# Attention scores from split operands: three one-pass products, with the keys split a batch ahead on ScalarE and GpSimd

## What is computed

```python
x = x + jnp.tanh(g_xattn[0]) * _L0_xattn_ref(_layernorm(x, axis=-1), ctx_1024, ...)
x = x + jnp.tanh(g_ffn[0]) * _L0_ffn_ref(_layernorm(x, axis=-1), ...)
x = x + jnp.tanh(g_xattn[1]) * _L1_xattn_ref(_layernorm(x, axis=-1), ctx_1024, mask_BxS2_bf1, ...)
x = x + jnp.tanh(g_ffn[1]) * _L1_ffn_ref(_layernorm(x, axis=-1), ...)
```

```python
sim = jnp.einsum('bhid,bhjd->bhij', q, k) * scale
attn = jax.nn.softmax(sim, axis=-1)
out = jnp.einsum('bhij,bhjd->bhid', attn, v)
...
return out @ Wo + bo
```

## Time and profile before

| | |
|---|---|
| median of three runs | 1489.21 us |
| span of the profiled execution, first to last instruction | 1487.2 us |
| the profiled execution's own time beyond its span | not listed; median less span is 2.0 us |
| PE busy | 1444.1 us, 97% of the span |
| DVE, ACT, POOL busy | 72%, 62%, 43% |
| granted TensorE clock, mean | 0.999 of full speed |
| first attention, feed-forward, second attention, spiking block | about 15 to 614, to 738, 749 to 1349, to 1487 us |

### The profile page before, as it was taken

How to read it: one execution, slowest core, us unless ns; L and a number is a source line. 1 busy time by engine, 2 the same in 40 slices (tenths; PEclk the granted TensorE clock), 3 DMA queues, 4 the chain that set the end, 5 groups by cost and what they waited for, 6 DMA issues and landing times. The chain is left out here.

```text
span 1487.2 us, 27490 instructions
## 1 busy us (share of the span) xinstructions
PE 1444.1 (97%) x9366; PEld 1209.9 (81%) x9384; DVE 1064.9 (72%) x2311; ACT 923.1 (62%) x1924; POOL 640.4 (43%) x755
## 2 busy tenths in 40 slices
PE   9999999999999999879999999999999999999997
PEld 8888888888888887639978888888888888778886
DVE  5677877666767678798566666666767676776887
ACT  4666666666666665496456666666666666556663
POOL 1333344343433334556023434343333333455885
PEclk9999999999999999999999999999999999999999
DMA  7655544444444442300055444444444444320011
GB/s 226 192 178 161 165 132 153 137 145 144 140 146 138 153 130 85 91 1 1 12 183 165 135 157 133 157 129 161 134 159 132 154 129 151 109 79 8 29 35 43
DMA packets 202786, 182.70 MB, mean 123 GB/s; under 512 B 12368, under 2 KB 201808, under 8 KB 202640
## 3 DMA queue, kind: packets, MB, share of 16 engines
q1 hardware_dynamic: 202080, 180.91, 38.7%
q10 hardware_dynamic: 576, 0.13, 0.1%
HBM read 95.74 MB, written 85.25 MB: 122 GB/s over the span
## 5 line engine op out<-in xcount | busy, mean ns | idle before, releaser
L1131 POOL TENSOR_TENSOR PN<-E,RC 128x512 f32<-128x512 f32 x378 | 331.2, 904 | 491.9 <-DVE RC L1089 491.9
L1038 DVE TENSOR_REDUCE MX<-pS 128x6 f32<-128x462 f32 (+1 forms) x384 | 222.6, 580 | 265.4 <-PE pS L657 265.4
L772 ACT ACTIVATE G<-pP 128x308 f32<-128x308 f32 (+1 forms) x488 | 208.9, 428 | 226.8 <-PE pP L525 226.5
L695 PE MATMUL pO<-work,PT 128*128 128x128 f32 (+1 forms) x2560 | 328.3, 276 | 4.1 <-ACT PT L856 4.1
L657 PE MATMUL pS<-G,XT 128*128 128x462 f32 (+1 forms) x768 | 321.0, 507 | 0.0
L695 PEld LDWEIGHTS pO<-work,PT 128*128 128x128 f32 (+1 forms) x2560 | 307.7, 192 | 8.4 <-issue 5.8
L847 ACT ACTIVATE E<-E 128x462 f32<-128x462 f32 (+1 forms) x384 | 209.6, 546 | 136.5 <-DVE E L1048 128.2
L523 PE MATMUL pP<-Chi,Ahi 128*128 128x308 f32 x496 | 235.2, 474 | 1.4 <-ACT G L772 1.2
L1048 DVE TENSOR_TENSOR E<-pS,MX 128x462 f32<-128x462 f32 (+1 forms) x384 | 223.6, 582 | 8.9
L856 ACT ACTIVATE PT<-pT 128x512 f32<-128x512 f32 (+1 forms) x384 | 200.2, 522 | 30.2 <-PE pT L680 28.7
L1086 DVE TENSOR_REDUCE SM<-E 128x16 f32<-128x1232 f32 (+1 forms) x144 | 184.8, 1290 | 44.7 <-ACT E L847 43.6
(11 more groups left out here) (241 smaller groups left out, 2032.7 us busy)
## 6 DMA issues: line engine op xcount, KB each, us to landing
values<-ST SPq DMA_DIRECT2D x256, 256.0 KB
work<-values SPq DMA_DIRECT2D x512, 128.0 KB
values<-ST SPq DMA_DIRECT2D x64, 208.0 KB
work<-values SPq DMA_DIRECT2D x128, 104.0 KB
C<-in_ctx SPq DMA_DIRECT2D x32, 154.0 KB
X<-in_x SPq DMA_DIRECT2D x16, 256.0 KB, 5.0
out<-s_O SPq DMA_DIRECT2D x16, 256.0 KB, 2.3
work<-in_L_xattn_Wq SPq DMA_DIRECT2D x2, 512.0 KB, 5.9
```

The lines of the kernel that those rows point to most:

```text
L695: last = nc.tensor.matmul(pO[:, 0:CH], PT[0:rows, c, :], V[(t - 1) % VRING][0:rows, tile, CH * hh:CH * hh + CH], start=c == 0, stop=c == C ...
L772: return nc.scalar.activation(G[0:live, g % 2, :, head, :], bank[0:live, 0:KEYCOLS].rearrange("p (b k) -> p b k", k=KEYS), ACT.Copy)
L1038: nc.vector.tensor_reduce(MX[:, h0:h1], pS[u][:, 0:(h1 - h0) * KEYS].rearrange("p (h k) -> p h k", k=KEYS), X_AXIS, ALU.max).then_inc(max_ ...
L1131: nc.gpsimd.tensor_tensor(out, e, scale, ALU.mult).then_inc(prob_ready, 1)
```

## The change

- **Scores.** Each f32 score matmul becomes three f32r matmuls into the same bank: `XThi` by `Ghi`, `XTlo` by `Ghi`, `XThi` by `Glo`. The first waits for `ghi_out`, the last for `glo_out`.
- **Keys split.** `G` stays f32 and is filled as before. New buffers `Ghi` and `Glo` hold one batch. ACT copies each unit of the next batch into `Ghi` (`keys_hi`), behind the same unit's exponential in slot t; POOL subtracts (`keys_lo`) at the head of its slot, ahead of the probabilities. In the fourth slot of a group the third unit comes after the last key's copy, and after the tiling of the context on POOL.
- **x split.** The copy of the turned x goes to f32r `XThi`, and DVE subtracts `XTlo` once in a group, in its third slot.
- **Contexts.** The ring of raw contexts has two places (`RAW`); contexts 2 and 3 are loaded once 0 and 1 are turned, behind the query and key weights and two loads of x. In the loop the load of a context waits for the turn of the one two before it.
- **Room.** `XTlo` of the first layer lies in the buffer of the spiking weights, and `WT` in that of `WP`. The DMA that places the mask's row in `G` (second layer) waits for `glo_out` in place of `score_ready`.

```diff
 def load_context(sp, c, dram, g):
-    sp.dma_start(c["C"][0:KEYS, g % CTX, :, :], dram[g * GROUP:(g + 1) * GROUP].rearrange("b k d -> k b d")
-                 ).then_inc(c["c_in"][g % CTX], 16)
+    sp.dma_start(c["C"][0:KEYS, g % RAW, :, :], dram[g * GROUP:(g + 1) * GROUP].rearrange("b k d -> k b d")
+                 ).then_inc(c["c_in"][g % RAW], 16)
...
-            for g in range(CTX):
+            for g in range(RAW):
                 sp.wait_ge(sem["padded"], g + 1)
                 load_context(sp, ctx, ctx_dram, g)
...
+            for g in range(RAW, CTX):
+                sp.wait_ge(ctx["ct_turned"], g - RAW + 1)
+                load_context(sp, ctx, ctx_dram, g)
...
                     if u == 0 and b == 0:
                         pe.wait_ge(xt_out, group + 1)
-                        wait(pe, made_out, MADE[t])
+                        pe.wait_ge(xt_low, group + 1)
                     wait(pe, shifted, (t - 1) * 3 + u + 1)
                     h0, h1 = UNITS[u]
                     out = pS[u][:, 0:(h1 - h0) * KEYS]
-                    if layer == 1 and u == 0 and b == 0:
-                        pe.wait_ge(bias_in[half], 16 * (group // 2 + 1))
-                    nc.tensor.matmul(out, XT[:, half, b, :], G[:, half, b, h0:h1, :].rearrange("p h k -> p (h k)"),
-                                     start=True, stop=True).then_inc(score_ready, 1)
+                    hi, lo = (c[:, h0:h1, :].rearrange("p h k -> p (h k)") for c in (Ghi, Glo))
+                    pe.wait_ge(ghi_out, t * 3 + u + 1)
+                    nc.tensor.matmul(out, XThi[:, half, b, :], hi, start=True, stop=False)
+                    nc.tensor.matmul(out, XTlo[:, half, b, :], hi, start=False, stop=False)
+                    pe.wait_ge(glo_out, t * 3 + u + 1)
+                    nc.tensor.matmul(out, XThi[:, half, b, :], lo, start=False, stop=True).then_inc(score_ready, 1)
...
+            def keys_hi(t, u):
+
+                (h0, h1), b, group = UNITS[u], t % GROUP, t // GROUP
...
+                wait(act, score_ready, (t - 1) * 3 + u + 1)
+                nc.scalar.activation(Ghi[:, h0:h1, :], G[:, group % 2, b, h0:h1, :], ACT.Copy).then_inc(ghi_out, 1)
...
+                def next_hi(u):
+                    if t + 1 < BATCH:
+                        keys_hi(t + 1, u)
+
                 produced(0)
                 produced(1)
                 produced(2)
                 exps(0)
+                next_hi(0)
...
                 produced(3)
                 exps(1)
+                next_hi(1)
                 produced(4)
                 probs_out(0)
                 produced(5)
                 exps(2)
+                if b < GROUP - 1:
+                    next_hi(2)
                 probs_out(1)
                 produced(6)
+                if b == GROUP - 1:
+                    next_hi(2)
                 probs_out(2)
...
+            def x_low(g):
+                dve.wait_ge(xt_out, g + 1)
+                nc.vector.tensor_tensor(XTlo[:, g % 2, :, :].rearrange("p b q -> p (b q)"), pO[:, :],
+                                        XThi[:, g % 2, :, :].rearrange("p b q -> p (b q)").bitcast(F32),
+                                        ALU.subtract).then_inc(xt_low, 1)
...
+            def keys_lo(t, u):
+
+                if t < BATCH:
+                    h0, h1 = UNITS[u]
+                    pool.wait_ge(ghi_out, t * 3 + u + 1)
+                    nc.gpsimd.tensor_tensor(Glo[:, h0:h1, :], G[:, (t // GROUP) % 2, t % GROUP, h0:h1, :],
+                                            Ghi[:, h0:h1, :].bitcast(F32), ALU.subtract).then_inc(glo_out, 1)
...
             for t in range(BATCH):
                 b, group = t % GROUP, t // GROUP
                 nxt = group + 1 < GROUPS
+                keys_lo(t + 1, 0)
+                keys_lo(t + 1, 1)
+                if b < GROUP - 1:
+                    keys_lo(t + 1, 2)
```

More of the change, by code:

```diff
@@ L36 @@
 CTX = 4
+RAW = 2
 FC = FF // 128
@@ L98, in context_buffers @@
          "Vlo": s.enter_context(nc.sbuf_tensor(f"Vlo_{layer}", [128, 2, OCTET], F32R))}
-    c["c_in"] = [s.enter_context(nc.semaphore(f"c_in{i}_{layer}")) for i in range(CTX)]
+    c["c_in"] = [s.enter_context(nc.semaphore(f"c_in{i}_{layer}")) for i in range(RAW)]
     for n in ("ct_turned", "chi_out", "clo_out", "tiled"):
@@ L266, in _ @@
         def _(dve):
-            for i in range(CTX):
+            for i in range(RAW):
                 nc.vector.memset(ctx["C"][:, i, :, :], 0.0).then_inc(sem["padded"], 1)
@@ L355, in attention @@
         XN = sb("XN", [128, GROUP, CH])
-        XT = sb("XT", [128, 2, GROUP, QUERIES])
+        XThi = sb("XThi", [128, 2, GROUP, QUERIES], F32R)
+        XTlo = p["F"][:, :, :].rearrange("p i (b q) -> p i b q", q=QUERIES) if layer == 0 else sb(
+            "XTlo", [128, 2, GROUP, QUERIES], F32R)[:, :, :, :]
+        Ghi, Glo = sb("Ghi", [128, HEADS, KEYS], F32R), sb("Glo", [128, HEADS, KEYS], F32R)
         BN = sb("BN", [128, GROUP, 6])
@@ L426, in attention, with key_made @@
             MADE.append(MADE[-1] + len(products(t)))
+        def key_made(first, head):
+            t = first + head // 4
+            return MADE[t] + products(t).index(("key", head)) + 1
         def probabilities(t, n):
@@ L739, in slot @@
                         pe.wait_ge(xt_out, group + 2)
+                        pe.wait_ge(xt_low, group + 2)
                     if b == 3 and cur and group + CTX < GROUPS:
@@ L767, in x_out @@
                 act.wait_ge(xt_turned, g + 1)
-                nc.scalar.activation(XT[:, g % 2, :, :].rearrange("p b q -> p (b q)"), pO[:, :],
+                nc.scalar.activation(XThi[:, g % 2, :, :].rearrange("p b q -> p (b q)"), pO[:, :],
                                      ACT.Copy).then_inc(xt_out, 1)
+            def keys_hi(t, u):
+                (h0, h1), b, group = UNITS[u], t % GROUP, t // GROUP
+                if t == 0:
+                    for i in range(2):
+                        act.wait_ge(first_out[i], (BLOCKS + h1) // 2)
+                elif b == 0:
+                    act.wait_ge(made_out, key_made(t - GROUP, h1 - 1))
+                if layer == 1 and b == 0 and u == 0:
+                    act.wait_ge(bias_in[group % 2], 16 * (group // 2 + 1))
+                wait(act, score_ready, (t - 1) * 3 + u + 1)
+                nc.scalar.activation(Ghi[:, h0:h1, :], G[:, group % 2, b, h0:h1, :], ACT.Copy).then_inc(ghi_out, 1)
             def keys_out(bank, g, head):
@@ L834, in produced @@
                         if b == 0 and j == 0:
-                            wait(act, score_ready, t * 3)
+                            wait(act, glo_out, t * 3)
                         act.wait_ge(made, m + 1)
@@ L1068, in slot @@
                     context_lo(nc, ctx, pO, group + CTX)
+                if b == 2 and nxt:
+                    x_low(group + 1)
                 row_max(2)
@@ L1159, in _ @@
                 tile_context(nc, pool, ctx, g)
+            for u in range(3):
+                keys_lo(0, u)
             add_bias(0)
@@ L1827, in program @@
                    "WOUT": f.enter_context(nc.sbuf_tensor("WOUT", [128, FC, CH], F32)),
+                   "WT": spiking["WP"],
                    "inv": f.enter_context(nc.sbuf_tensor("inv", [128, 2, FC], F32))}
```

34 lines of the change are left out of this document (22 added, 12 removed).

## The result

The change takes 1582.03 us (median of four runs, 1580.45 to 1583.56) against 1488.69 before: the ratio is 1.063, with a 95% interval of 1.0617 to 1.0644. The forecast was 1583 in a range of 1557 to 1606. The profiled execution spans 1578.6 us, 91.4 more than before.

What follows compares the result with a forecast made beforehand. TensorE bounded the kernel, but ScalarE's chain would take over: +0.8 us a slot, 47 us a layer, 94 for both, taking the span from 1487.2 to 1581.2; with 2.0 for the median, 1583 us, range 1557 to 1606.

Steps and rivals of the forecast that it cites:

- What bounds the kernel before: Attention slots: TensorE's own work sets the 9.18 us slot, with the ScalarE chain close behind.
- The 0.12 us: Slot 28 before the change: time the ScalarE chain has to spare, slot end 307.13 against 307.01.
- the 1.72: Slot 28: us from the end of the second turned-probabilities copy to the slot's end, 0.38 plus 1.34.
- The gain on TensorE: Score matmuls: three f32r passes replace f32, 1.70 for 2.09 us; 0.39 us a batch, 50 us for 128.
- The copies: ScalarE: three SBUF copies add 1.33 us ahead of the second turned-probabilities copy; a 0.23 hole leaves 1.10.
- The sum for a slot: Seven-product attention slot along the ScalarE chain: 3.25 + 5.03 + 1.72 = 10.00 us against 9.18, +0.8 us.
- The total: Whole kernel: both attention layers add 94 us, profiled span 1581.2, median 1583 us.
- The faster rival: Attention: TensorE stays the limit, slot 8.79 us, time 1439 us; chance 0.08.
- The GpSimd rival: Attention: GpSimd's subtractions hold up probabilities and scores from 2 us each, 25 us more, 1608 us; chance 0.05.
- The expected waits: Attention, TensorE: waits for `PT`, `ST` and `G` on ScalarE, tens of us in total.

Runs made afterwards that it cites:

- e4: Changed kernel reordered: ScalarE's first copy ahead of the first exponential, other two behind the last turned-probabilities copy, GpSimd's last two subtractions just ahead of the probabilities: 1467.07 us.
- e5: Changed kernel with only the second and third units' copies moved behind the last turned-probabilities copy, GpSimd's last two subtractions just ahead of the probabilities: 1500.36 us.
- e3: Changed kernel with scores again one f32 product from G, using only x's high part; copies, subtractions and waits kept, two waits added: 1598.18 us.
- e2: Changed kernel with GpSimd subtracting only 8 of each head's 77 keys after the first batch: 1582.89 us.
- e7: Changed kernel with GpSimd making every subtraction twice, the second waiting for the first: 1667.55 us.
- e1: Changed kernel with the three ScalarE copies left in place but copying 8 of each head's 77 keys after the first batch: 1489.94 us.

## Why the prediction held, point by point

- **What bounds the kernel before.** Held: TensorE's work, with ScalarE's chain close behind it. The 0.12 us rest on the 1.72 from the copy's end to the slot's; it is 1.65 us in the change and 1.66 in e4, where slot 28 of the kernel before had 307.13 - 305.29 = 1.84. That puts the room at 0.19. In e4 and e5 the slots shrink as soon as the chain has more.
- **The gain on TensorE.** 0.21 us a pass was forecast for 462 columns, 0.21 measured. TensorE's work was forecast at 8.79 us a slot; the slot of e4 is 8.85, of which some 0.05 is still a wait for ScalarE.
- **The copies.** 0.49, 0.50 and 0.35 forecast from the exponentials of the same shapes, 0.48, 0.48 and 0.35 measured.
- **The sum for a slot.** To the first exponential 3.25 forecast, 3.27 measured (323.63 less 320.36). From there to the end of the copy 5.03 and 4.98. From there to the end of the slot 1.72 and 1.65. Together 10.00 and 9.90 us, the last two terms a little on the high side: +0.8 was +0.72.
- **The total.** +94 us forecast, +91.4 measured between the profiled spans. The first layer's attention grew by some 47 us, the second's by 44. Here two misses cancel in part, which is luck: in the steady part an octet grew by 5.9 us where 6.2 were laid out, the last nine slots of a layer by 4.8 and 4.9 where 4.2 were.
- **The faster rival** (TensorE stays the limit) fell: in e3 50 us of TensorE's work came back and cost 16. The Trainium skill's rule to optimise the engine of highest occupancy first ("Perfetto Trace Analysis", Identifying the Most-Contended Engine) named TensorE at 97%, and its work did shrink; the trace disagrees that this decides, since the chain behind it had 0.1 to 0.2 us to spare. The same section of the Trainium skill says of TensorE that its busy share is not a good measure of how close it is to its limit; here too a share of 96% hid a slot that was 1.05 us longer than need be, as the last point shows.
- **The GpSimd rival** fell for this change (e2) and showed up when forced (e7), by the tiling of the context and the clock behind it, and not by each slot's scores. The forecast held that in the attention only the normalising of x would meet GpSimd; e1 and e2 show a second one, the statistics of the next block (`rs_after`).
- **Wrong in detail.** TensorE was to be busy near 88% of a window; it is 96%. A stalled matmul is drawn as a longer record, not as a gap: the L547 row above ends 0.61 us behind the transposes, 0.38 later than in a full stream, and only 0.10 of that is a gap between records. The expected waits are there, but the waits view shows 46 us for `pO` and 9 for the product banks, while 9.90 less 8.85 is 1.05 us in each slot like slot 28. The longer records hide most of the stall, and some of it stands in the rows of the weight loads, which overlap them. GpSimd's subtractions were to take 970 and 650 ns and took 1178 and 841. The term was scaled from a product of the same engine and was too small by a fifth; e2 shows that it did not matter.

## What to carry to other kernels

When an engine is full, look for the next chain before taking work off it: from the slot's start through the waits to the last instruction that releases it, and subtract. Here less than 0.2 us were to spare. With 1.33 us of copies in the wrong place the kernel became 93 us slower, although TensorE had less to do; with the same copies in the holes of the same engine it became 21 us faster. Work for a later slot belongs where its engine waits, and the timeline of that engine shows these holes; the place in the list is worth more than the engine's busy share.

## What the runs showed that was not expected

- GpSimd's subtraction into f32r takes 1178 ns for 462 columns, longer than its product into f32 for 512 (1082). In the spiking block a subtraction into f32 took 1164 ns at the median for 512 columns, between the two by the column; whether the operation, the operands or the output type does it was not tried.
- A ScalarE copy of 48 columns takes 234 ns from start to end and holds the engine for 130, one of 462 columns for 480: a copy made ten times shorter costs a quarter.
- VectorE's normalising of x, one line, before and with the change (ns min/median/max):

```profile
L932 DVE TENSOR_SCALAR XN<-X,MV,RS x128: 334/340/345, 27.5 to 1295.7; 128x128 f32<-128x128 f32 x64, 128x127 f32<-128x127 f32 x64
```

```profile
L977 DVE TENSOR_SCALAR XN<-X,MV,RS x128: 329/339/1341, 27.4 to 1384.9; 128x128 f32<-128x128 f32 x64, 128x127 f32<-128x127 f32 x64
```

About one in each group of four batches (28 of the 128) now takes some 1260 ns, and up to 1341. Each of these began within 0.1 us of the start of a subtraction on GpSimd and ended some 0.08 us behind its end; in e2, with the subtractions short, the longest is 347 ns. The Trainium skill ("SBUF — State Buffer", Who interferes with whom) lists a tensor-with-scalar instruction in a 2-port mode among those that share a pair of ports with GpSimd, one fully blocking the other; the trace agrees, since the time is that of a whole subtraction (1178 ns) and a little more. It cost no time that e2 could find, unlike the same meeting at `rs_after` in e1.
